# A decoder layer on one core: the output weight loads of batch 0 issued at another step, and the merge order written anew

## Chip, core and metric

One core of one Trainium2 chip. The metric is the device time of one execution in microseconds (us). Engines: PE (TensorE, matmuls), DVE (VectorE), ACT (ScalarE), POOL (GpSimd), SP (the queue that issues most DMAs).

## The reference

For 4 batches of 256 tokens by 256 channels, one decoder layer, with a layer norm behind each of its three parts:

```
x = layernorm(x + attn(x, Wqkv, Wo))        # 16 heads of 128, 2 kv heads, rotary, tanh softcap, causal
x = layernorm(x + xattn(x, ctx, mask, ...)) # 16 heads of 16, q and o projections quantised to 8 bits
x = layernorm(x + ffn(x, Wr, br, W1, W2))   # router keeps 4 of 16 blocks per token, gelu
```

## The kernel before

Each batch is cut into small operations, and they are grouped in seven streams, each in its own fixed order: `r` (rotate: split of x and weights, `rot` 0 to 8, that is k and eight pairs of q heads), `s` (scores: `near` j for each pair of heads, `far` for every two pairs), `m` (`val`, `mix` 2j and 2j + 1 for pair j, `turn` j, `proj` j, and in batch 0 `wo` n, at the end `norm1`), `c` (context, and in batch 0 `quant_w`, `turn_w` and `w1`), `x` and `y` (cross-attention of the two token tiles: `quant_x`, `turn_x`, `query`, `turn_q`, `xscore`, `turn_p`, `xmix`, `turn_o`, `quant_o`, `turn_ox`, `outproj`), `n` (`turn_z`, `route`, `turn_m`, `hidden`, `ffn`). The string `ORDER` of 531 letters merges the streams; `make_plan` takes the next operation of the stream that each letter names. Every engine, SP too, walks through the same plan and issues its own part of each operation, so the string sets the order on all of them at once. An engine waits on semaphores in that order and never passes a waiting instruction.

Work of batches overlaps: while self-attention of batch b + 1 runs, cross-attention and the network of batch b fill in.

The PE writes to 7 PSUM banks in turn (`claim`): an operation takes the bank that was used seven uses before, once that one is released by ACT or DVE. The output projection of pair j, `proj` j, adds to a bank of its own, `acc` (12 matmuls, line 585).

The output weights `Wo` come in eight parts, one for each pair. In batch 0 a part is loaded as plain f32 into one of three buffers `wo_f` (these lie in `xs`, so the profile shows the load as `xs<-in_wo`, 256 KB, line 374). At `wo` n ACT rounds it to `wo_s` (line 888), POOL takes the rest (line 1354), and SP stores both to DRAM (`wo_parts`, 512 KB, line 387), from where later batches load them. The rounding of part n (n from 3) waits for the load of part n, for the store of part n - 3 and for `proj` n - 3. The load of part n + 3 waits for the rest of part n. In the stream, `wo` 0 to 2 stand at the start and `wo` n + 3 stands right behind `proj` n.

Rotary in batch 0 is done with DVE reading across halves. From batch 1 on, DVE writes two products (lines 1046, 1047), SP swaps halves by two DMAs (line 398), and POOL adds (line 1348). POOL also does the causal masks (line 1366) and the power in each layer norm (line 1377). Line 1250 is DVE's router. Line 442 loads `W1` (1 MB).

Of the kernel before, what the change touches and what calls it, by code (L numbers as in the profile page):

```python
# [36 lines left out]
B, T, C = 4, 256, 256  # L37
# [3 lines left out]
PAIRS = NH // 2  # L41
# [15 lines left out]
WO_SLOTS, WO_FLAT = 3, 3  # L57
# [70 lines left out]
def network_ops(b):  # L128
# [16 lines left out]


ORDER = (
    "rrrrrmsmrmssrrmrrmsmmrssmsmrmmmmmmmrmssrrrmmmmmmcsssmmmmmccmmmmrrmcccccmmmcmrcmmrsrmcccssmcmmmrmmsmssrxmm"
    "rrmmmsyssmmmxmsmyxmmmmxyssmmrmmymmyyrrmymxxmmrxxxxyymmmrryxyxsxxmxyyymmyyxxxxsyyysrryxxxyymmxymxxmmsccmmx"
    "msscxyrcccxmmssrsyxmmmmmmsyxrmmmmmyyxssmmxrrxxmxmmmmmyxrynmmmrxxxyxxrxxsxyyxxmmmsyysyymmxyyyxyrynyxyysyrn"  # L150
    "xyyymmmxmxynyymcxnyxxsscnnxynccccmxmsmrxmsyxryxmxxsxxmyxsxxxxnynmxxyymxxmxyyxyyxmnxyyysyxyxmmyyyymmxyyyxs"
    "ymcymymmmmmymmymmcmmcccmmncnnnyynxxyxnyxyxnynxyxxxxxyyyyyxxxxyyyyxxxyyyxyxyyxxnyxyyxxnnnynxynxnnnnnnnnnnn"
    "nnnnnn")


# [33 lines left out]
def build_decoder(nc, x, xT, ctxT, mask, wqkv, wo, wkvT, xwq, xwo, xbias, wrT, br, w1T, w2T,  # L189
# [10 lines left out]
    with ExitStack() as ctx:  # L200
# [114 lines left out]
        def wait_for(eng, name, b, i=0, t=0):  # L315

            if b >= 0:
                eng.wait_ge(sig[name, t], count(name, b, i))
# [8 lines left out]
        def wait_filled(eng, kind, b, i=0, t=0, k=0):  # L327

            if b >= 0:
                eng.wait_ge(filled, where[kind, b, i, t, k] + 1)  # L330


        tiles = [(k, i) for k, _, i, _ in score_ops(0)]
        tile_at = {t: n for n, t in enumerate(tiles)}

# [22 lines left out]
        def _(sp):  # L358
            rows = lambda a: a.rearrange("(k p) n -> p k n", p=P)
            def load_tokens(b):  # L360
                if b == 1:
                    sp.wait_ge(quant_w, 14)
                for t in range(TT):
                    wait_for(sp, "ln2", b - 2, 1, t)
                sp.dma_start(y1[:, b % 2], rows(x[b])).then_inc(xtok_in[b % 2], 16)

            def load_wo(b, j):

                n = b * PAIRS + j
                slot = n % WO_SLOTS  # L370
                if b == 0:
                    if j >= WO_FLAT:
                        sp.wait_ge(wo_lo, j - WO_FLAT + 1)
                    sp.dma_start(wo_f[:, j % WO_FLAT], rows(wo)[:, 2 * j:2 * j + 2, :]).then_inc(wo_flat[j % WO_FLAT], 16)
                else:
                    wait_for(sp, "projected", *divmod(n - WO_SLOTS, PAIRS))
                    first = j % WO_SLOTS
                    if b == 1:
                        sp.wait_ge(wo_out[first], 16 * (j // WO_SLOTS + 1))
                        if slot != first:  # L380
                            sp.wait_ge(wo_out[slot], 16 * len(range(slot, PAIRS, WO_SLOTS)))
                    sp.dma_start(wo_s[:, slot].rearrange("p a m c -> p (a m c)").bitcast(F32), wo_parts[j]).then_inc(wo_in[slot], 16)

            def store_wo(j):

                sp.wait_ge(wo_lo, j + 1)
                sp.dma_start(wo_parts[j], wo_s[:, j % WO_SLOTS].rearrange("p a m c -> p (a m c)").bitcast(F32))\
                    .then_inc(wo_out[j % WO_SLOTS], 16)

            def swap_halves(b, i):  # L390

                n = b * (PAIRS + 1) + i
                lower, upper = slice(0, HD // 2), slice(HD // 2, HD)
                if n >= 2:
                    sp.wait_ge(sig["rotated", 0], n - 1)
                wait_for(sp, "roped", b, 3 * i)
                for dst, src in ((lower, upper), (upper, lower)):
                    sp.dma_start(rope_s[dst, n % 2], rope_t[src, n % 2]).then_inc(swapped[n % 2], 16)

            def load_context(b):  # L400
                wait_filled(sp, "ctx", b - 1, 1)
                sp.dma_start(ctx_s[:], rows(ctxT[b])).then_inc(ctx_in, 16)

            def load_mask(b):
                for t in range(TT):
                    wait_for(sp, "xmasked", b - 1, 4 * QUADS - 1, t)
                sp.dma_start(mask_s[:], rows(mask[b])).then_inc(mask_in, 16)
# [4 lines left out]
            for n in range(1, PIECES):  # L412
                sp.dma_start(raw[n], rows(wqkv[:, (n - 1) * PW:n * PW])).then_inc(piece_in[n], 16)
            sp.dma_start(ident_s[:], ident).then_inc(ident_in, 16)
            for j in range(WO_SLOTS):
                load_wo(0, j)
            load_tokens(0)
            for w, a in enumerate((xwq, xwo)):
# [9 lines left out]
            for kind, b, i, t in plan:  # L428

                done.add((kind, b, i, t))  # L430
                both = all((kind, b, i, n) in done for n in range(TT))
                if kind == "rot" and b:
                    swap_halves(b, i)
                elif kind == "rot" and i == 2 * PLAIN - 1:
                    wait_filled(sp, "rot", 0, 2 * PLAIN - 2)
                    wait_filled(sp, "val", 0)
                    wait_for(sp, "x_lo", 0)
                    sp.dma_start(xT_s[:], rows(xT[1])).then_inc(x_in, 16)
                elif kind == "rot" and i == PAIRS:
                    for n in range(PLAIN, PIECES):  # L440
                        sp.wait_ge(piece_lo[n], 2)
                    sp.dma_start(w1_f[:], rows(w1T)).then_inc(w1_in, 16)
                elif kind == "quant_w" and i == 1:
                    load_tokens(1)
                elif kind == "wo":
                    store_wo(i)
                elif kind == "proj" and b * PAIRS + i + WO_SLOTS < B * PAIRS:
                    load_wo(*divmod(b * PAIRS + i + WO_SLOTS, PAIRS))
                elif kind == "outproj" and both and b + 2 < B:
                    load_tokens(b + 2)  # L450
                elif kind == "ctx" and i == TT - 1 and b + 1 < B:
                    load_context(b + 1)
                elif kind == "xscore" and i == QUADS - 1 and both and b + 1 < B:
                    load_mask(b + 1)
                elif kind == ("last" if b == B - 1 else "ffn"):
                    wait_for(sp, "ln3", b, 4, t)
                    sp.dma_start(out[b, t * P:(t + 1) * P, :], y3[:, t, :]).then_inc(sig["stored", t], 16)
# [983 lines left out]
```

## Time and profile before

| | us |
|---|---|
| median of 3 runs | 398.35 (396.69 to 400.66) |
| profiled execution | 400.16 |
| its span, first to last instruction | 398.4 |
| PE busy | 376.6 (95%) |
| PE weight loads busy | 322.9 (81%) |
| DVE busy | 299.9 (75%) |
| ACT busy | 247.2 (62%) |
| POOL busy | 148.8 (37%) |
| mean granted TensorE clock | 0.994 of full |

The span is that of the profiled execution, and 1.8 us of its time lie outside it. Busy time of PE is modelled from its pipelined matmuls and can hide gaps shorter than one matmul.

### The profile page before, as it was taken

The page shows a single profiled execution, that of the slowest core. Times are in us where ns is not written, and L with a number is a line of the kernel's source. Part 1 is how long each engine was busy: PE and PEld are TensorE (multiplying, and loading weights), DVE is VectorE, ACT ScalarE, POOL GpSimd, SP SyncE. Part 2 cuts the span into 40 slices and gives each one's busy share as a digit, 9 for nine tenths or more (in the row PEclk, how much of TensorE's full clock was granted, in tenths as well). Part 3 has the DMA queues.
Part 4 walks back from the last instruction along what each step waited for, and adds up shares of the span by engine and source line. Part 5 has one row for each costly group of instructions (what it writes and reads, how often), then busy time and mean ns, then how long its engine had stood idle before and what let it go on. Part 6 is the DMA issues. An engine that isn't in the chain of part 4 may idle for free.

```text
span 398.4 us, 9013 instructions
## 1 busy us (share of the span) xinstructions
PE 376.6 (95%) x3038; PEld 322.9 (81%) x3038; DVE 299.9 (75%) x900; ACT 247.2 (62%) x526; POOL 148.8 (37%) x173
## 2 busy tenths in 40 slices
PE   7989998999999999998999999999999988899893
PEld 6768886878899988787998896888888877679783
DVE  2998998758778687878887888897888687777603
ACT  1666545644676984555579847598983439984230
POOL 6598545546824604245553122142113321000101
PEclk9999999999999999999999999999999999999999
DMA  7981554644335433033444110130123000000000
GB/s 266 369 294 44 171 169 149 199 150 91 119 107 134 129 112 81 26 107 128 129 143 132 30 54 28 41 105 9 62 81 100 8 2 20 8 3 2 26 2 26
DMA packets 21404, 38.42 MB, mean 96 GB/s; under 512 B 2544, under 2 KB 12144, under 8 KB 21360
## 3 DMA queue, kind: packets, MB, share of 16 engines
q1 hardware_dynamic: 20272, 36.80, 29.8%
q10 hardware_dynamic: 1088, 1.05, 0.8%
q8 instruction: 26, 0.43, 0.5%
q14 instruction: 18, 0.15, 0.1%
HBM read 25.52 MB, written 5.24 MB: 77 GB/s over the span
## 4 chain that ended last, share of the span: by engine, by line
PE 74%; DVE 7%; DMA 5%; ACT 4%; POOL 4%; issue 3%; SPq 1%; POOLq 0%; DVEq 0%; ACTq 0%
PE bank L479 10%; PE acc L585 9%; PE bank L671 7%; PE bank L552 5%; PE bank L732 5%; PE bank L529 5%; PE bank L752 5%; PE bank L683 4%; PE bank L660 4%; PE bank L611 4%; PE bank L566 3%; PE bank L555 3%; DMA rope_s<-rope_t 2%; PE bank L537 2%; DMA xs<-in_wo 2%
## 5 line engine op out<-in xcount | busy, mean ns | idle before, releaser
L914 ACT ACTIVATE xs<-xs,xneg 128x256 f32<-128x256 f32 x128 | 54.4, 500 | 9.1 <-DVE xneg L1191 8.8
L1359 POOL TENSOR_TENSOR a_lo<-a_flat,a_hi 128x512 fp32r<-128x512 f32 x32 | 41.6, 1302 | 26.7 <-ACT a_flat L829 26.7
L1377 POOL TENSOR_TENSOR small<-small,half 128x1 f32<-128x1 f32 x24 | 13.2, 550 | 101.6 <-DVE small L1077 101.6
L585 PE MATMUL acc<-wo_s,a_hi 128*128 128x256 f32 x256 | 49.8, 293 | 0.7 <-POOL a_lo L1359 0.6
L1191 DVE CUSTOM_DVE_ANT_0 xs<-bank,mask_s 128x256 f32<-128x256 f32 x128 | 46.3, 419 | 3.0 <-PE bank L660 2.7
L1348 POOL TENSOR_TENSOR q_T<-q_T,rope_s 128x512 f32<-128x512 f32 x24 | 30.8, 1285 | 45.6 <-DMA rope_s<-rope_t 45.4
L552 PE MATMUL bank<-v_s,p_near 128*128 128x129 f32 x256 | 41.7, 277 | 2.8 <-POOL p_far L1366 1.8
L585 PEld LDWEIGHTS acc<-wo_s,a_hi 128*128 128x128 f32 x256 | 39.3, 189 | 4.0 <-POOL a_lo L1359 2.8
L552 PEld LDWEIGHTS bank<-v_s,p_near 128*128 128x128 f32 x256 | 35.2, 191 | 6.7 <-issue 4.8
L479 PE MATMUL bank<-x_hi,wqkv_hi 128*128 128x256 f32 x124 | 37.6, 304 | 0.2 <-DVE q_T L1047 0.2
L585 PE MATMUL acc<-wo_s,a_lo 128*128 128x256 f32 x128 | 35.9, 281 | 0.0
L671 PE MATMUL bank<-ident_s,xs 128*128 128x128 f32 x256 | 35.2, 277 | 0.4 <-ACT xs L914 0.3
L479 PE MATMUL bank<-x_lo,wqkv_hi 128*128 128x256 f32 x124 | 34.9, 282 | 0.0
L479 PE MATMUL bank<-x_hi,wqkv_lo 128*128 128x256 f32 x124 | 34.8, 281 | 0.0
L671 PEld LDWEIGHTS bank<-ident_s,xs 128*128 128x128 f32 x256 | 28.3, 141 | 7.1 <-issue 6.2
L829 ACT CAST a_hi<-bank 128x512 fp32r<-128x512 f32 x32 | 18.8, 586 | 23.5 <-PE bank L566 23.2
L529 PE MATMUL bank<-q_T,k_T 128*128 128x512 f32 x64 | 32.8, 602 | 0.3
L870 ACT ACTIVATE p_near<-bank 128x512 f32<-128x512 f32 x32 | 19.1, 598 | 20.3 <-PE bank L529 20.0
L1200 DVE COPY xp_T<-bank 128x512 f32<-128x512 f32 x32 | 21.9, 688 | 10.2 <-PE bank L671 9.9
L829 ACT CAST qS<-bank 64x256 fp32r<-64x256 f32 x64 | 23.3, 363 | 9.4 <-PE bank L648 8.5
L1067 DVE TENSOR_TENSOR a_s<-bank,a_rec 128x256 f32<-128x256 f32 x64 | 27.2, 425 | 2.2
L660 PE MATMUL bank<-kS,qS 128*128 128x256 f32 x128 | 23.8, 309 | 2.4 <-ACT qS L829 1.5
(169 smaller groups left out, 999.0 us busy)
## 6 DMA issues: line engine op xcount, KB each, us to landing
wo_s<-wo_parts SPq DMA_DIRECT2D x24, 512.0 KB, 3.4
rope_s<-rope_t SPq DMA_DIRECT2D x54, 128.0 KB, 2.3
wo_parts<-wo_s SPq DMA_DIRECT2D x8, 512.0 KB, 3.7
xs<-in_wo SPq DMA_DIRECT2D x8, 256.0 KB, 5.7
stage<-in_wqkv SPq DMA_DIRECT2D x2, 512.0 KB, 6.3
xp_T<-in_wqkv SPq DMA_DIRECT2D x2, 512.0 KB, 8.0
y<-in_x SPq DMA_DIRECT2D x4, 256.0 KB, 3.0
ctx_s<-in_ctxT SPq DMA_DIRECT2D x4, 256.0 KB, 2.8
```

The source lines that it names most:

```text
L479: ins = mm(ps, lhs[i], rhs[j], start=(k == 0 and n == 0), stop=(last and n == 2))
L529: mm(ps[:, :], k_T[:, j // 4, 0:P], q_T[:, j % 4].rearrange("p h q -> p (h q)"), start=True, stop=True).then_inc(filled, 1)
L552: ins = mm(o, p_near[:, j % NEAR, m, t * P:(t + 1) * P], v_s[:, 0, j // 4, :], start=True, stop=(t == 0))
L585: ins = mm(acc[:, t, :], a[x], wo_s[:, slot, w, m, :], start=(j == 0 and t == 0 and m == 0 and p == 0), stop=(j == PAIRS - 1 and m == 1 an ...
L660: ins = mm(ps[m][:, m2 * T:(m2 + 1) * T], qS[:, t, m2, m, :], kS[:, g, m2, :], start=True, stop=True)
L671: ins = transpose(ps[:, m2 * T + k * P:m2 * T + (k + 1) * P], xs[:, t, m, m2, k * P:(k + 1) * P], ident_s[:])
L829: copy(dst, src).then_inc(sig[name, t], 1)
L914: activation(xs[:, t, m, m2, :], xs[:, t, m, m2, :], ACT.Exp, bias=xneg[:, t, m, m2:m2 + 1], scale=-1.0)\
L1067: v.tensor_tensor(a_s[:, j % 2, t], ps[:, :, 0:HD], rec.to_broadcast([P, 2, HD]), ALU.mult)\
L1191: do(v.tensor_tensor_reduce(out=xs[:, t, m, m2, :], in0=bank("xscore", b, g, t, m)[:, m2 * T:(m2 + 1) * T], in1=mask_s[:, t, :], scale=-1. ...
L1348: g.tensor_tensor(dst, dst, (rope_s if b else rope_t)[:, n % 2], ALU.add).then_inc(sig["rotated", 0], 1)
L1359: g.tensor_tensor(a_lo[:, j % 2], a_flat[:, j % 2], a_hi[:, j % 2].bitcast(F32), ALU.subtract)\
```

## The change

In batch 0, SP issues the load of part n + 3 in the operation `wo` n, just behind the store of part n, and no longer in the operation `proj` n. The loads of batches 1 to 3 stay at `proj`. The first three loads are issued at the start as before (`WO_FLAT` and `WO_SLOTS` are both 3). No instruction is added or removed, and no wait. `ORDER` is written anew with the same number of each letter.

```
 ORDER = (
-    "rrrrrmsmrmssrrmrrmsmmrssmsmrmmmmmmmrmssrrrmmmmmmcsssmmmmmccmmmmrrmcccccmmmcmrcmmrsrmcccssmcmmmrmmsmssrxmm"
+    "rrrrrmsmrmssrmrrsrmmmmrsssmrrmmssmmmrmmrmmsrmmmmmmmmsscmmmrrccmmmmmrmmcmcccccmmrrcssmmmsmmrrmcmmsssxmcmrr"
...
-            for j in range(WO_SLOTS):
+            for j in range(WO_FLAT):
                 load_wo(0, j)
...
                 elif kind == "wo":
                     store_wo(i)
-                elif kind == "proj" and b * PAIRS + i + WO_SLOTS < B * PAIRS:
+                    if i + WO_FLAT < PAIRS:
+                        load_wo(0, i + WO_FLAT)
+                elif kind == "proj" and PAIRS <= b * PAIRS + i + WO_SLOTS < B * PAIRS:
                     load_wo(*divmod(b * PAIRS + i + WO_SLOTS, PAIRS))
```

All five long lines of the string differ. Read through `make_plan`, the operations of batch 0 behind the first projection stand as follows (`b.i` is batch and index):

```
before: proj0.0 wo3 mix6 mix7 piece1 turn2 near5 far2 rot8 piece2 split_x1 proj1 wo4 mix8 mix9 turn3 proj2
        quant_w0 near6 near7 far3 wo5 mix10 mix11 turn4 proj3 turn_w0 quant_w1 wo6 mix12 mix13 turn5 rot1.0
        rot1.1 proj4 turn_w1 w1 x4 wo7 mix14 mix15 ctx0 turn6 rot1.2 ctx1 proj5 turn7 rot1.3 near1.0 rot1.4
        proj6 turn_k0 turn_k1 turn_k2 near1.1 far1.0 proj7 turn_k3 norm1 norm1 val1 rot1.5 ...
after:  proj0.0 wo3 rot8 mix6 mix7 piece2 turn2 proj1 near6 split_x1 wo4 mix8 mix9 turn3 proj2 wo5 mix10
        mix11 near7 far3 quant_w0 turn4 proj3 wo6 rot1.0 rot1.1 turn_w0 quant_w1 mix12 mix13 turn5 proj4 wo7
        rot1.2 mix14 mix15 turn_w1 turn6 w1 x4 ctx0 proj5 turn7 rot1.3 rot1.4 ctx1 near1.0 near1.1 proj6
        proj7 norm1 far1.0 norm1 val1 rot1.5 ...
```

In batches 1 to 3 operations move by a few places each. Near the end, `route` and `turn_m` of batch 2 move forward: before, `route` stood behind the last `turn_p` of batch 3 and `turn_m` behind both `quant_o`; after, `route` stands behind the third `xscore` of one tile of batch 3 and `turn_m` right behind the last `turn_p`. From `outproj` of batch 3 on the two orders are alike.

## Rows read from the trace of the kernel before

**Rows 1.** Busy time by stretch; columns as in the first line.
```profile
core 0: us, PE busy (x) PEld busy (x) DVE busy (x) ACT busy (x) POOL busy (x), PEclk, DMA share, GB/s
8.24:34.38 26.14, 24.88 (x135) 19.14 (x135) 23.12 (x37) 14.73 (x27) 20.09 (x18) 1.00 0.84 289
34.38:57.80 23.42, 22.73 (x167) 19.81 (x168) 21.60 (x43) 14.58 (x27) 14.92 (x14) 1.00 0.40 135
57.80:98.98 41.18, 38.94 (x260) 31.30 (x258) 30.87 (x69) 19.98 (x37) 21.61 (x23) 1.00 0.50 149
98.98:312.01 213.03, 211.82 (x1863) 184.03 (x1863) 170.61 (x557) 151.15 (x335) 78.61 (x90) 1.00 0.30 88
...
325.50:355.40 29.90, 26.02 (x248) 21.56 (x246) 22.89 (x89) 25.47 (x64) 1.10 (x2) 1.00 0.03 10
355.40:376.40 21.00, 18.92 (x160) 17.03 (x158) 14.80 (x58) 8.60 (x18) 2.19 (x4) 1.00 0.02 7
376.40:398.40 22.00, 15.51 (x90) 13.99 (x90) 4.50 (x22) 4.31 (x8) 1.09 (x2) 0.90 0.06 19
```

**Rows 2.** The chain that ended last, batch 0: start, us, what.
```profile
39.13 1.54 SPq L442
...
40.71 6.48 DMA xs<-in_wo
...
47.22 0.63 ACT wo_s L888
...
55.12 2.84 PE bank L479 x24
```

**Rows 3.** Waits, whole span: us in total, times, longest.
```profile
ACT wo_s L888 <- DMA xs<-in_wo: 14.7, 4, 5.3
```

**Rows 4.** Timeline of PE: start, us, and idle before in brackets.
```profile
50.48 0.50 PE L585 MATMUL acc<-wo_s,a_hi 128*128 128x256 f32 x2 [0.55 <-POOL a_lo L1359]
...
62.61 1.98 PE L611 MATMUL bank<-wkv_s,ctx_s 128*128 128x512 f32 x4 [1.16 <-ACT a_flat L829]
...
78.15 0.80 PE L585 MATMUL acc<-wo_s,a_hi 128*128 128x256 f32 x2
```

**Rows 5.** Timeline of SP: the DMAs as issued.
```profile
18.91 8.18 SPq L387 DMA_DIRECT2D wo_parts<-wo_s  x3
...
27.64 0.79 SPq L374 DMA_DIRECT2D xs<-in_wo  x1
```

**Rows 6.** Timeline of DVE, batch 0.
```profile
47.32 0.68 DVE L1093 TENSOR_REDUCE q_amax<-z 128x2 f32<-128x512 f32 x1
...
58.21 0.48 DVE L1117 TENSOR_SCALAR q_tmp<-ident_s,q_scale 128x128 f32<-128x128 f32 x2
...
63.59 2.92 DVE L1233 TENSOR_TENSOR w_lo<-xp_T,w_hi 128x512 fp32r<-128x512 f32 x4 [1.11 <-ACT w_hi L930]
```

**Rows 7.** The chain that ended last, start of batch 1.
```profile
74.89 0.70 DVE rope_t L1046
...
76.16 4.29 DMA rope_s<-rope_t
...
84.44 0.53 POOL small L1377
...
91.51 0.44 PE bank L566 x4
...
99.14 1.54 PE acc L585 x12
```

**Rows 8.** The chain that ended last, its end part.
```profile
355.41 0.81 PE bank L710 x8
356.25 0.17 DVE prob L1250
...
358.36 0.19 DVE keep L1266
...
376.39 4.59 PE bank L732 x24
```

More of the change, by code:

```diff
@@ L147 @@
 ORDER = (
-    "rrrrrmsmrmssrrmrrmsmmrssmsmrmmmmmmmrmssrrrmmmmmmcsssmmmmmccmmmmrrmcccccmmmcmrcmmrsrmcccssmcmmmrmmsmssrxmm"
[L149 to L152, printed above, removed]
+    "rrrrrmsmrmssrmrrsrmmmmrsssmrrmmssmmmrmmrmmsrmmmmmmmmsscmmmrrccmmmmmrmmcmcccccmmrrcssmmmsmmrrmcmmsssxmcmrr"
+    "rcmmmscssmxymmmmmyxmmsysmxsyxmmmmrrmxmmyyxxryyyxxmmmmmymyxxxyyyyxxxymmmmxmysxxssryyrryxxxsymymxycrsxxmmsm"
+    "rcxmmxxmmsccccssyrrymmxmmmsmyxsmymsmmymxmmmrmyxrmxmxxxmyxxmmmrynmyyrxxysxyxyymmxyxxmmsysyyxyxyrrmmxxyyyrn"
+    "xyysymmxysxyyccxnmnnyxncynsxmnxcccxsymmsxsmxmxmxmxyxxrxyxxxnxyxnsyyxxmxmmyyyryxyyxxyyynxyymmyyxmxssmmmmxy"
+    "yyxmymmymymmcymmycmmmmnccyccnnnyxnyxxnxyxynynyxxyyyxxyyyynxxxxyyyxxxyyyxxxyyxxxnyxyynxnynxxynxnnnnnnnnnnn"
     "nnnnnn")
```

## The prediction

> **What bounds the kernel now.** I read the busy time of each engine by stretch first, then the chain that ended last, then the waits of ACT and PE in batch 0, then SP's issues. The stretches [rows 1] show PE idle for 1.2 of 213.0 us between the first projection of batch 1 (98.98) and the last two of batch 3 (312.01). Idle time elsewhere is 1.3 us up to 34.38, 0.7 up to 57.80, 2.2 up to 98.98, and 3.9, 2.1 and 6.5 in the last three stretches. So the time is PE's work, plus what PE loses in batch 0, plus what it loses behind the last projection.
>
> Busy time can hide short gaps, so I also added up PE's work along the plan, at the duration that an undisturbed group of each kind has in the chain: 0.12 us for a matmul of a rotation or a projection (24 in 2.84 [rows 2]), and likewise for the others. PE's first real matmul starts at 8.24. Against this sum PE is 0.6 us late at projection 0 of batch 0 (34.38 [rows 1]), 1.4 at projection 3 (50.48 [rows 4]), 3.8 at projection 7 (78.15 [rows 4]), 5.6 at projection 0 of batch 1 (99 [rows 7]), and 4.7 at the last projection of batch 3 (the difference of 0.9 is the error of the sum). So some 5.0 us are lost between 34 and 99, nothing that I can see from 99 to 312, and the rest behind it.
>
> The Trainium skill (Perfetto Trace Analysis, Identifying the Most-Contended Engine) says that matmul busy time is a bad measure of how full TensorE is, and that weight load busy time should be taken. By that, the middle has 29 us of room (184.0 of 213.0), and a better order could win some of it there. The sum of the plan's work speaks against it here, and only a small chance below rests on it.
>
> **The loads.** ACT waits four times for a part of the output weights, 14.7 us in all [rows 3]. The worst case is in the chain [rows 2]: behind the store of part 3 the load of W1 holds SP for 1.54 us from 39.13, the load of part 4 lands 6.48 us after 40.71, ACT rounds at 47.22, and projection 3, whose input was queued on ACT behind that rounding, starts at 50.48 [rows 4]. After the change, loads 3, 4 and 5 go out behind stores 0, 1 and 2, that is between 19 and 27; before, load 3 went at 27.64 [rows 5], load 4 at 40.7 and load 5 after it. Load 6 goes out behind store 3 (about 39) and ahead of W1, load 7 behind store 4 (about 45). Roundings 4 to 7 are due at about 43, 46, 51 and 58, right behind projections 1 to 4. Each load then has 6 us or more, so this wait goes, all 14.7 us of it.
>
> What the loads collide with: the DMA engines are 84% busy up to 34 [rows 1], so the three early loads land later than one alone would, and delay the x of batch 1, which no engine reads before 40. The price is between 0 and 2 us of a transfer with over 10 us to spare; I take 0. SP's queue gets no new wait: the load needs the same rest of part n that the store just before it waited for.
>
> **What PE gets of it.** ACT is not the bound. PE itself idled only 0.55 us ahead of projection 3 and 1.16 us ahead of the first context product, whose bank was held by ACT's late copy [rows 4]. DVE idled 1.11 us for ACT's late rounding of W1 [rows 6]. The direct gain is 0.55 + 1.16 = 1.7 us.
>
> What is late next is DVE. Up to 57.80 it is busy 21.6 of 23.4 us [rows 1]. The two quantisations of weights, some 5 us each, lie between 47.32 and 58.7 [rows 6], and everything on DVE behind them waits. In the new order two rotations of batch 1 (1.2 us each) come ahead of the second one, and mix 12 and 13 follow it. Counted on from the measured end of mix 9, DVE ends quantisation 1 at about 61.0 and mix 13 at 62.1, while PE asks for them at 60.4 and 61.0. PE waits some 1.1 us there, with 0 and 2.5 us as bounds: 2.5 if both added rotations (2.4 us) come on top. Before, that place cost nothing.
>
> Then the start of batch 1. Before, rotation 3 runs on DVE at 74.89, its swap lands 4.29 us after the issue at 76.16, POOL adds, masks, and only then does the first power of layer norm 1 at 84.44 [rows 7]; the norm holds DVE, rotation 5 follows, and its bank holds PE, which comes to turn 0 of batch 1 at 91.51 [rows 7]. This is where PE goes from 3.8 to 5.6 us late. In the new order rotation 2 stands 6.9 us of DVE work earlier, ahead of the W1 rest and the context, projections 6 and 7 come together (at about 74 to 75.5 in place of 78.2), and fewer operations lie between projection 7 and the norm. Counting the same steps: rotation 4 on DVE ends at 73 to 75, its swap and POOL's addition at 79 to 81.3, the power at 80.2 to 82.5 in place of 84.44, and PE reaches turn 0 of batch 1 at 88 to 90, where it was at 91.51 with 0.9 us more work behind it. That is 0.6 to 2.6 us less lost. I take the middle, **1.6 us**, for the whole of batch 0; the bounds with full success or none are 5.0 and 0.
>
> **The first 34 us.** The new order moves near 2 ahead of rotation 6 and a weight split ahead of mix 4. DVE is busy 23.1 of 26.1 us there [rows 1], and its work up to projection 0 is 2.0 us more, PE's is 1.7 us more. I take 0, bounds 1 us either way.
>
> **The middle, 99 to 312.** The same work, and PE has nothing to win. It can lose: the shortest distance between a rotation and its first score, in PE work, was 6.8 us from batch 1 on, and is now 5.8 and 5.9 us in batch 2, while the chain of rotation, swap, addition takes 6 to 8 us by [rows 7]. Bounds 0 and 1.9, I take 0.3, since in the trace the waits of this kind leave PE idle for only 1.2 us in all of this stretch.
>
> **The end.** From 325.5 to 355.4 ACT is busy 25.5 of 29.9 us, the fullest engine but PE, and PE idles 3.9 us [rows 1]. The route of batch 2 now comes into this stretch. Its PE part (0.81 us [rows 8]) fits into PE's idle time, and what PE lost to the router by the sum of its work, 0.76 us, is gone from 358: 1.6 us, less 0.5 us since the last mix now follows its copy more closely, gives 1.1. In return the router's DVE steps, 356.25 to 358.55 [rows 8], and ACT's two small exponentials (between DVE's steps, some 0.5 us) come into the busy stretch: between 0.5 us (only ACT's part) and 4.0 us (2.3 us of DVE, and 1.7 us in which DVE waits for four exponentials ahead of the router's on ACT). I take 1.1, so 0 in sum, with bounds -0.6 and +2.9. The clock is another term: 24 matmuls of batch 3's network took 4.59 us at 376.39 against 2.84 for as many at full clock, and the granted clock is 0.90 in this stretch against 1.00 before [rows 1, 2, 8]. PE had idled 2.1 of the 21.0 us ahead of it. The end of the order is unchanged, so I take it as it is, 1.75 us either way.
>
> **The sum.** -1.6 + 0.3 = -1.3 us against the profiled execution of 400.16 (its span of 398.4 and 1.8 around it), which makes 398.9; that execution is 1.8 above the median, so against the median of 398.35 it makes **397.0 us**.
>
> **Rivals.**
> - The wait moves to DVE. The loads are early, but the quantisations and the two rotations ahead of mix 12 cost what the loads gave (the 2.5 bound), and the norm is reached no sooner. For it: DVE's 21.6 of 23.4 us. Against it: rotations 2 to 4 do come earlier. It gives 398.35. To it belongs the case that the change doesn't do what it says (a load still last at a rounding), which gives the same time.
> - All of batch 0's loss goes. -5.0, and -1.1 at the end if the route is hidden: 392.3. For it: every chain through ACT is shorter by 4 to 5 us, and the rotations of batch 1 by more. Against it: DVE's load. The skill's rule of room in the middle is part of this case.
> - Slower: the router of batch 2 on DVE, ahead of the scores of batch 3. Its price is up to +2.9 us net, and it decides from the point where the early gain is below it. With the gain at its least, 0, and 1 us in the first stretch or the middle, this makes 398.35 + 3.9 = 402.2; with the forecast gain, 399.9.
>
> **How the numbers follow.** Forecast 0.46 (own range 395.5 to 398.0), wait moved to DVE 0.20, all gone 0.20, slower 0.14. The range leaves out 2 in 10: from 392.3 with half of the second rival at its end to 401.2, between the two times of the third: 392.5 to 401.2. A measurement here tells some 1% from no change (4 us; three runs spread over 4.0). Faster by over 1%, below 394.4, is nearly all of the second rival and a tail of the forecast: 0.22. Slower by over 1%, above 402.3, needs the third at its full price: 0.08. Within 1%: 0.70.
>
> **What would show it.** Loads of parts 3 to 5 on SP before 28; ACT's wait for them gone; projection 3 starting at about 49.7; no idle time ahead of the first context product, but some 1 us at turn 6 or turn_w 1, released by DVE; the first power of norm 1 near 81; projection 0 of batch 1 at about 97.4; the middle as long as before; ACT's stretch ahead of 355 longer and the router's wait at 358 gone. I am wrong if PE's idle time in batch 0 doesn't shrink, if the middle has waits of several us, or if the end grows by more than 2 us.

## The result and the profile after

The changed kernel takes 393.85 us (median of 6 runs, 392.26 to 395.3), the kernel before on the same chip 397.88 (6 runs, 396.57 to 400.66). The ratio is 0.9896, 95% interval 0.9866 to 0.9927: 4.0 us faster. The forecast was 397.0, in a range of 392.5 to 401.2 that holds the result. The sign was right; the gain was forecast at 1.3 us, a third of what came. The result lies below the forecast's own range (395.5 to 398.0) and in that of the second rival, all of batch 0's loss gone, which had a chance of 0.20.

The profiled execution of the changed kernel took 395.3 us, its span is 393.6. Busy time by stretch answers to [rows 1]. The first two stretches are cut at the times of [rows 1], not at events (in this execution PE starts at 9.22 and projection 0 of batch 0 at 37.71); 96.66 is projection 0 of batch 1, 308.03 the last two projections of batch 3, and the last line is the end part. In the kernel before, the last two projections start at 311.45, so the fourth line of [rows 1] is 0.56 us longer than this one's counterpart:

```profile
8.24:34.38 26.14, 24.82 (x119) 18.66 (x120) 21.73 (x35) 14.24 (x26) 17.84 (x17) 0.93 0.91 309
34.38:57.80 23.42, 23.42 (x180) 20.89 (x179) 21.03 (x44) 15.57 (x29) 18.23 (x16) 1.00 0.41 147
57.80:96.66 38.86, 38.35 (x263) 31.37 (x262) 33.13 (x78) 19.61 (x36) 21.84 (x23) 1.00 0.50 144
96.66:308.03 211.37, 211.14 (x1862) 183.81 (x1861) 165.93 (x548) 149.34 (x333) 77.49 (x88) 1.00 0.30 87
...
372.00:393.60 21.60, 14.20 (x92) 12.59 (x92) 5.58 (x26) 5.16 (x9) 1.09 (x2) 0.96 0.06 19
```

PE has no idle time at all between 34.38 and 57.80, where it had 0.7 us, and 0.5 us from there to batch 1, where it had 2.2. ACT works 15.6 us in that stretch where it worked 14.6, and POOL 18.2 where it worked 14.9: both have done more by 57.80 (ACT 29.8 against 29.3 us, POOL 36.1 against 35.0). The view of waits has no line in which ACT's rounding waits for a load [rows 3]. SP's timeline shows why, and answers to [rows 5]:

```profile
21.43 0.34 SPq L387 DMA_DIRECT2D wo_parts<-wo_s  x1
21.81 0.43 SPq L374 DMA_DIRECT2D xs<-in_wo  x1
...
25.32 0.44 SPq L374 DMA_DIRECT2D xs<-in_wo  x1
...
29.62 1.06 SPq L374 DMA_DIRECT2D xs<-in_wo  x1
...
43.14 0.43 SPq L374 DMA_DIRECT2D xs<-in_wo  x1
43.67 0.78 SPq L442 DMA_DIRECT2D xp_T<-in_w1T  x1
```

Loads 3, 4 and 5 go out at 21.8, 25.3 and 29.6, each behind a store, and load 6 goes ahead of W1. PE's timeline has one wait between 34 and 97, and none at turn_w 1. The kernel before has four: 0.55 and 1.16 us [rows 4], and two at the start of batch 1, 0.74 at 84.58 (for POOL's mask of `far`) and 0.20 at 88.93:

```profile
65.80 0.50 PE L587 MATMUL acc<-wo_s,a_hi 128*128 128x256 f32 x2 [0.44 <-POOL a_lo L1361]
```

In the chain of work that ended last, the first power of norm 1, the last piece ahead of projection 0 of batch 1, and the 24 matmuls of batch 3's network answer to [rows 7] and [rows 8]:

```profile
80.26 0.53 POOL small L1379
...
96.37 0.86 PE bank L539 x2
...
373.08 3.04 PE bank L734 x24
```

Against the same sum of PE's work as in the prediction, PE is now 2.3 us late at projection 0 (37.71), 2.3 at projection 3 (51.29), 3.2 at projection 5 (65.80), 3.3 at projection 0 of batch 1 (96.66). So 1.0 us is lost between these two ends, where the kernel before lost 5.0.

The changed execution began badly: its first weights let PE start at 9.22, not 8.24, and the granted clock is 0.93 up to 34 (1.00 before). In two other runs that share its first operations (e3, e11 below) PE starts at 8.13 and 8.34, and projection 0 stands at 35.07 and 35.28. The span before was 398.4, so the 4.8 us between the spans are +1.7 (start), -4.0 (34 to batch 1), -1.1 (middle, 211.4 against 212.5), -1.4 (end, where the 24 matmuls above are 1.55 us shorter than 4.59 [rows 8]).

The profiled execution of the kernel before is 2.3 us above its median, that of the changed kernel 1.5 above its own. So e1 below, which has the time and the order of the kernel before, is the fairer trace to compare with.

### The profile page after: what moved, and what is told of

It reads as the page before. It is cut to its first block, busy times and chain, and to the rows that moved or that the text cites. A ratio compares the mean times of both kernels' runs of the same rounds, so it can differ in the third digit from the quotient of the medians.

```text
span 393.6 us, 9011 instructions
## 1 busy us (share of the span) xinstructions
PE 376.1 (96%) x3038; PEld 322.4 (82%) x3038; DVE 295.4 (75%) x900; ACT 245.4 (62%) x524; POOL 149.8 (38%) x173
## 4 chain that ended last, share of the span: by engine, by line
PE 75%; DVE 9%; DMA 5%; issue 3%; POOL 3%; ACT 3%; SPq 1%; POOLq 0%; DVEq 0%; ACTq 0%
PE acc L587 9%; PE bank L481 8%; PE bank L673 6%; PE bank L554 6%; PE bank L734 6%; PE bank L531 6%; PE bank L754 5%; PE bank L685 4%; PE bank L662 3%; PE bank L568 3%; PE bank L557 3%; DMA rope_s<-rope_t 3%; PE bank L539 3%; PE bank L613 2%; PE bank L500 2%
## 5 line engine op out<-in xcount | busy, mean ns | idle before, releaser
L1048 DVE TENSOR_TENSOR rope_t<-bank,sin_s 128x512 f32<-128x512 f32 x27 | 18.6, 688 | 10.9 <-PE bank L481 6.3
```

## The experiments

All are whole kernels timed in five rounds, with ratios to the kernel before. `ORDER` is shown as operations. Lines of kernels with the early loads stand two below those of before.

**e1: the loads alone.** The order of before, the loads of the changed kernel.

```
 ORDER = (the string before)
+                    if i + WO_FLAT < PAIRS:
+                        load_wo(0, i + WO_FLAT)
```

> The merge order of before, with the loads of parts 3 to 5 issued behind the first stores. Theory A (the gain of 4 us needs both parts: PE loses some 4 us less between 34 and 99, of which only the waits for ACT belong to the loads): 1.7 us faster than before, ratio 0.996, within 0.993 to 0.999; ACT no longer waits for a load, the idle 0.55 and 1.16 us of PE are gone, DVE's quantisations still hold mix 10 and 11. Rival B (the loads alone do it): ratio 0.990. Rival C (the order alone does it): ratio 1.000.

Measured 398.05 us, ratio 1.0008 (0.9979 to 1.0037). Nothing is gained: the time that rival C named, and below what the loads should have given by theory A. ACT waits for no load any more, and the idle times ahead of projection 3 and of the first context product are gone. In their place stand two that the kernel before did not have, at turn_w 0:

```profile
52.68 0.38 PE L599 MATMUL bank<-identb_s,q_int 128*128 128x128 bf16 x4 [1.31 <-DVE q_int L1106]
54.09 0.68 PE L605 MATMUL bank<-q_tmp,ones 128*128 128x128 f32 x4 [1.02 <-DVE q_tmp L1119]
```

PE is stopped by quantisation 0 on DVE: it got 1.71 us and paid 2.33. DVE and POOL side by side, same execution:

```profile
49.12 0.37 DVE L1097 TENSOR_SCALAR q_scale<-q_amax 128x2 f32<-128x2 f32 x1
...
51.16 1.37 DVE L1106 TENSOR_SCALAR q_int<-q_tmp 128x512 bf16<-128x512 f32 x1
52.57 1.37 DVE L1119 TENSOR_SCALAR q_tmp<-ident_s,q_scale 128x128 f32<-128x128 f32 x2
...
57.39 0.43 DVE L1104 TENSOR_SCALAR q_tmp<-q_tmp 128x512 f32<-128x512 f32 x1
```

```profile
50.82 1.44 POOL L1356 TENSOR_TENSOR wo_s<-xs,wo_s 128x512 fp32r<-128x512 f32 x1
52.22 1.44 POOL L1361 TENSOR_TENSOR a_lo<-a_flat,a_hi 128x512 fp32r<-128x512 f32 x1
```

The two DVE instructions that lie beside POOL's take 1.37 us each; where POOL is idle the first kind takes 0.43 and the second 0.48 for both (changed kernel, 59.90 and 60.36). In the kernel before, too, a pair of POOL's rests (weights, then attention) lies on quantisation 0, at 47.91 and 49.14. With the loads early that pair comes sooner and stretches the DVE instruction ahead of the quantisation instead, so that it starts 1.1 us later (48.41 against 47.32 [rows 6]), and the next pair, shown above, falls on its end:

```profile
45.67 1.75 DVE L1026 TENSOR_TENSOR x_lo<-xT_s,x_hi 128x512 fp32r<-128x512 f32 x1
```

```profile
45.16 1.71 POOL L1356 TENSOR_TENSOR wo_s<-xs,wo_s 128x512 fp32r<-128x512 f32 x1
46.83 1.72 POOL L1361 TENSOR_TENSOR a_lo<-a_flat,a_hi 128x512 fp32r<-128x512 f32 x1
```

In the kernel before, the same x_lo takes 0.68 us at 45.65, with POOL idle. Projections 3, 5 and 7 stand at 49.70, 67.61 and 78.17 here and at 50.48, 67.60 and 78.15 before: what is won ahead of projection 3 is lost at turn_w 0.

**e2: the order alone.** The order of the changed kernel, loads at the projection.

```
 ORDER = (the string after)
-                    if i + WO_FLAT < PAIRS:
-                        load_wo(0, i + WO_FLAT)
```

> The merge order of after, with the loads of batch 0 at the projections as before. Theory A: the roundings of parts 4 to 7 wait for loads again, and in this order projections 1 and 2 leave less time; most of the gain is gone, ratio 0.996 to 1.003. Rival B: 1.000. Rival C: 0.990, since the rotations and projections of the start of batch 1 still come earlier.

Measured 400.71 us, ratio 1.008 (1.0052 to 1.0108), slower. ACT waits 15.9 us for loads, and PE idles 1.67 us at 50.47 and 3.19 us at 68.83:

```profile
68.83 0.79 PE L585 MATMUL acc<-wo_s,a_hi 128*128 128x256 f32 x2 [3.19 <-POOL a_lo L1359]
```

So neither part gains alone, and together they gain 1.04%: the two need each other. Rival B falls with e1 and rival C with e2; theory A, that both parts are needed, stands, but not its figures, since by them the loads alone would have given 1.7 us.

**e3 and e4: where in the order.** e3 has the early loads, the first 158 operations of the new order and the rest of the old one; e4 is the changed kernel with its last 67 operations in the old order.

```
e3: ORDER = after[:158] + before[158:]
e4: ORDER = after[:464] + before[464:]
```

> Loads early, the order of after for the first 158 operations (up to projection 4 of batch 1), that of before from there on. Theory A: batch 0 holds nearly all of the gain, ratio 0.990 to 0.993. Rival D (the middle, where PE's idle time fell from 1.2 to 0.2 us, or the end gave part of it): ratio 0.994 or more, and less than after by over 1 us.

> The kernel of after, with only the last 67 operations (from turn_z of batch 2 on) in the order of before, so that the route of batch 2 stands behind the last turn_p again. Theory A (the moved route costs as much as it gives): same as after, ratio 0.990 with 0.5 us to either side. Rival D: the moved route helps, ratio 0.994; or it costs, as the slower rival of the prediction had it, ratio 0.985.

Measured 394.33 us, 0.9925 (0.9899 to 0.9952), and 394.27 us, 0.9918 (0.9892 to 0.9945). The start carries some three quarters of the gain. What is left, 0.3% to the middle and the end together (e3) and 0.2% to the end alone (e4), lies within the intervals.

**e5 and e6: finer.** Early loads with the first 57 operations (to projection 3) or 83 operations (to near 0 of batch 1) of the new order.

```
e5: ORDER = after[:57] + before[57:]
e6: ORDER = after[:83] + before[83:]
```

> Loads early, the order of after for the first 57 operations (up to projection 3 of batch 0; the first quantisation stands behind mix 11 in it), that of before from there on. Theory A2 (with early loads PE is held by DVE's first quantisation, between mix 9 and mix 10, and its turn_w; the gain is in the place of that and of the rotations, in batch 0): PE no longer idles 2.3 us at turn_w 0; ratio 0.996. Theory D2 (the start of batch 1 or later gives it all): 1.000, as with the loads alone.

> Loads early, the order of after for the first 83 operations (up to near 0 of batch 1, rotations 0 to 4 of batch 1 at their new places), that of before from there on. Theory A2: all of the gain but what the norm's new place gives: ratio 0.991 to 0.994. Theory D2: 0.998 or more.

Measured 396.44 us, 0.9945 (0.9917 to 0.9974), and 396.29 us, 0.9959 (0.9933 to 0.9984). Up to projection 3 the new order turns e1's nothing into half of the gain: quantisation 0 starts at 47.67 there instead of 48.41 and the two instructions that took 1.37 us each take 0.43 and 0.73, so PE idles 0.56 us at turn_w 0 in place of 2.33. e6 missed what was expected of it (0.991 to 0.994): the operations 58 to 83, with the rotations of batch 1 at their new places, give nothing more, and PE idles 0.49, 0.57 and 1.62 us there (63.31, 71.40, 74.70), the longest for DVE's `parts` (line 1151). The other 0.3% comes in the step from 83 to 158 operations (projections 6 and 7, the norm and the start of batch 1); the intervals of e6 and e3 overlap, and no run divides this step further.

**e7 and e8: only rotations moved.** On the early loads and the old order, e7 puts rotations 0 and 1 of batch 1 right behind projection 3, e8 puts rotation 2 right behind projection 4.

```
-proj3 turn_w0 quant_w1 wo6 mix12 mix13 turn5 rot1.0 rot1.1 proj4 turn_w1 ...
+proj3 rot1.0 rot1.1 turn_w0 quant_w1 wo6 mix12 mix13 turn5 proj4 turn_w1 ...       (e7)
-proj4 turn_w1 w1 x4 wo7 mix14 mix15 ctx0 turn6 rot1.2 ctx1 ...
+proj4 rot1.2 turn_w1 w1 x4 wo7 mix14 mix15 ctx0 turn6 ctx1 ...                     (e8)
```

> Loads early, the order of before, with only rotations 0 and 1 of batch 1 moved ahead of turn_w 0 and quantisation 1, so that PE has 2.8 us of other work while DVE quantises. Theory A2: the 1.3 and 1.0 us that PE idles at turn_w 0 with the loads alone go, some 1 us may come back where mix 12 and 13 now stand behind them on DVE: ratio 0.994 to 0.998. Theory D2: 1.000.

> Loads early, the order of before, with only rotation 2 of batch 1 moved ahead of turn_w 1, the rest of W1 and the context. If the late rotations (swap, POOL's addition, masks, the norm's power behind them) are what costs PE 1.8 us at the start of batch 1: ratio 0.996. If not, 1.000.

Both expectations failed: 402.63 us, 1.0099 (1.0061 to 1.0137), and 399.57 us, 1.0044 (1.0015 to 1.0073). In e7 the waits at turn_w 0 are gone as expected, but PE idles 5.56 and 0.81 us at turn_w 1, where only some 1 us was expected to come back. The DVE timeline of e7 over quantisation 1, and POOL's:

```profile
59.18 1.69 DVE L1102 TENSOR_SCALAR q_tmp<-y,q_rs 128x256 f32<-128x256 f32 x2
60.90 1.40 DVE L1104 TENSOR_SCALAR q_tmp<-q_tmp 128x512 f32<-128x512 f32 x1
62.33 1.37 DVE L1106 TENSOR_SCALAR q_int<-q_tmp 128x512 bf16<-128x512 f32 x1
63.74 1.36 DVE L1119 TENSOR_SCALAR q_tmp<-ident_s,q_scale 128x128 f32<-128x128 f32 x2
```

```profile
59.46 1.26 POOL L1350 TENSOR_TENSOR k_T<-k_T,rope_s 128x512 f32<-128x512 f32 x1 [5.59 <-DMA rope_s<-rope_t]
60.76 1.26 POOL L1350 TENSOR_TENSOR q_T<-q_T,rope_s 128x512 f32<-128x512 f32 x1
61.98 1.44 POOL L1356 TENSOR_TENSOR wo_s<-xs,wo_s 128x512 fp32r<-128x512 f32 x1
63.38 1.44 POOL L1361 TENSOR_TENSOR a_lo<-a_flat,a_hi 128x512 fp32r<-128x512 f32 x1
```

Four DVE instructions in a row take 1.4 to 1.7 us, each beside one of POOL's. The rotations sent their swaps off early, and POOL's additions came back 4.3 us later (from the first product on DVE at 55.14) on top of quantisation 1, which took 7.0 us (58.06 to 65.1) where the changed kernel takes 3.2 (57.66 to 60.84). My theory that the place of the rotations alone is the gain falls. e8 keeps e1's waits of 1.31 and 1.02 us at turn_w 0, and its clock is lower (0.94 from 34 to 58).

**e9: the suspected cost taken away.** e1, with POOL's instructions beside the quantisations made short: they compute 8 columns of each half of 256, and the kernel leaves out the rest, so its output is not the layer's.

```
+                n = 8 if j in (4, 5, 6) else C
+                g.tensor_tensor(s[:, 1, :, 0:n], wo_f[:, j % WO_FLAT, :, 0:n], s[:, 0, :, 0:n].bitcast(F32), ...
...
+                n = 8 if b == 0 and j in (3, 4, 5) else T
+                g.tensor_tensor(a_lo[:, j % 2, :, 0:n], a_flat[:, j % 2, :, 0:n], a_hi[:, j % 2, :, 0:n]...
```

> e1_loads_only with one thing left out: in batch 0 POOL's rests of output weight parts 4 to 6 and of attention pairs 3 to 5 are computed for 8 columns of each half in place of 256 (the other columns keep what stood in the buffer), so POOL's instructions of 1.27 to 1.72 us beside the two quantisations of weights shrink. No other engine has an instruction more or less, and the order is that of before. Theory (POOL's tensor-tensor work beside DVE stretches the quantisation, and PE waits for it at turn_w 0): the two DVE instructions that took 1.37 us each beside POOL's (quotient to integers, diagonal of scales) fall to about 0.5, quantisation 0 ends near 52 in place of 53.8, PE's 1.31 + 1.02 us ahead of turn_w 0 are gone, ratio to before 0.992 to 0.996. Rival (the quantisation is late by its place in the order, behind the split and the context of pair 3, and POOL is a bystander): its instructions keep their length, PE's wait stays near 2.3 us, ratio 0.999 to 1.002.

Measured 394.15 us, ratio 0.9914 (0.988 to 0.9948). The order is that of before to the letter, and 0.9% appears. PE has 0.1 us of idle time from 34 to 80, and 0.46 us from there to 98. The same DVE instructions and POOL's:

```profile
50.08 0.43 DVE L1106 TENSOR_SCALAR q_int<-q_tmp 128x512 bf16<-128x512 f32 x1
50.54 0.88 DVE L1119 TENSOR_SCALAR q_tmp<-ident_s,q_scale 128x128 f32<-128x128 f32 x2
```

```profile
51.11 0.22 POOL L1357 TENSOR_TENSOR wo_s<-xs,wo_s 128x16 fp32r<-128x16 f32 x1
```

Quantisation 0 ends at 51.4 in place of 53.9, quantisation 1 takes 3.2 us in place of 4.3. The trace accounts for some half of the gain: from projection 0 of batch 0 to that of batch 1 it takes 60.9 us against 62.9 in e1. The medians are 3.9 us apart, but this profiled execution, at 396.15, is the longest of its nine.

**e10: more cover for quantisation 1.** e7, with turn_w 1 and the W1 rest moved behind mix 15.

```
-turn5 proj4 turn_w1 w1 x4 wo7 mix14 mix15 ctx0 ...
+turn5 proj4 wo7 mix14 mix15 turn_w1 w1 x4 ctx0 ...
```

> e7_rot01_ahead with turn_w 1 and the split of W1 moved behind mix 15, as in the changed kernel, so that quantisation 1, which took 7 us there beside POOL's work, is not asked for by PE until some 5 us of PE work later. Theory (rotations 0 and 1 ahead of turn_w 0 pay once both quantisations have PE work to cover them): PE's idle of 5.56 + 0.81 us at turn_w 1 is gone or below 1 us, quantisation 0 is covered too, ratio 0.992 to 0.997. Rival (the rotations themselves, or POOL's additions of them, are what delays; cover only moves the wait to mix 12 to 15): PE idles several us at turn 6 or at a projection, ratio 1.002 to 1.010.

Measured 401.78 us, ratio 1.0109 (1.0055 to 1.0163). Missed. PE's wait at turn_w 1 is halved, not gone, and the time stays where the rival put it (1.002 to 1.010) or just above:

```profile
61.50 0.38 PE L599 MATMUL bank<-identb_s,q_int 128*128 128x128 bf16 x4 [1.22 <-DVE q_int L1106]
63.93 1.19 PE L605 MATMUL bank<-q_tmp,ones 128*128 128x128 f32 x4 [2.04 <-DVE q_tmp L1119]
```

Its last quantisation step takes 2.39 us at 61.39, beside POOL's additions at 61.19 and 62.44, and the granted clock is 0.92 from 57.8 to 80. Rotation 2 (24 matmuls, 2.84 us [rows 2]) stands ahead of turn_w 1 in the new order and not in e10; that it is the missing cover I argue from its length, no run shows it.

**e11: quantisation 0 put back.** The changed kernel, quant_w 0 ahead of wo 5 as before.

```
-proj2 wo5 mix10 mix11 near7 far3 quant_w0 turn4 proj3 ...
+proj2 quant_w0 wo5 mix10 mix11 near7 far3 turn4 proj3 ...
```

> The changed kernel with one operation moved back: quant_w 0 stands right behind projection 2, ahead of wo 5 and mix 10, as in the kernel before, in place of behind far 3. All of the rest is the changed kernel. Theory (what the new order gained in batch 0 hangs on where the quantisations fall beside POOL's rests): quantisation 0 grows from 3.9 towards 5 us, the mixes 10 and 11 and turn 4 come behind it, PE idles 1 to 2 us there, ratio to before 0.992 to 0.997, so 0.3 to 0.6% behind the changed kernel. Rival (the gain lies in the rotations and the start of batch 1): ratio 0.988 to 0.991, as the changed kernel.

Measured 394.5 us, ratio 0.9916 (0.9889 to 0.9944). Quantisation 0 grows to 4.6 us (46.08 to 50.64), but PE waits for it nowhere: the two rotations ahead of turn_w 0 cover it. Between the two theories' figures, and within the interval of the changed kernel: the place of this one operation is not the gain; by the two ratios 0.2% would hang on it, which the intervals do not show.

**e12: the same cost taken away from the changed kernel.** The edit of e9 on the new order.

```
 ORDER = (the string after)
+                n = 8 if j in (4, 5, 6) else C
+                n = 8 if b == 0 and j in (3, 4, 5) else T
```

> The changed kernel with the same thing left out as in e9_small_rests: POOL's rests of output weight parts 4 to 6 and attention pairs 3 to 5 of batch 0 computed for 8 columns of each half in place of 256. There, on the order of before, it took the ratio from 1.0008 to 0.9914. Theory (the new order has already moved the two quotations of time away: in it POOL's rests stand beside other DVE work, and PE waits for no quantisation): there is almost nothing left for it to win, ratio to before 0.986 to 0.990, at most 0.3% ahead of the changed kernel. Rival (smaller rests help by their own length, since a projection comes sooner after its rest, whatever the order): it wins here what it won there, ratio 0.979 to 0.983.

Measured 394.83 us, ratio 0.9928 (0.9901 to 0.9955), above the 0.986 to 0.990 of the theory and far from the rival. What was worth 0.9% on the old order is worth nothing on the new one (0.3% behind the changed kernel; the intervals overlap). That speaks against the reading that e9 gained because a projection comes sooner after a shorter rest. The traces give a reason why it may even cost a little: the store of part 6 no longer holds the swaps on SP, they go out at 52.70 instead of 56.81, and POOL's additions come back at 55.95 and 58.39, inside quantisation 1 (4.9 us, 55.08 to 59.98), and PE idles 0.46 us at turn_w 1 (60.58):

```profile
55.95 1.29 POOL L1350 TENSOR_TENSOR k_T<-k_T,rope_s 128x512 f32<-128x512 f32 x1 [3.99 <-DMA rope_s<-rope_t]
58.39 1.31 POOL L1350 TENSOR_TENSOR q_T<-q_T,rope_s 128x512 f32<-128x512 f32 x1 [1.15 <-DMA rope_s<-rope_t]
```

In the changed kernel they come at 62.01, just behind its end, because the store of part 6 holds SP until 56.7 (5.56 us for two stores from 51.15). The prediction did not count on that, so a part of the short quantisation 1 is luck:

```profile
62.01 1.27 POOL L1350 TENSOR_TENSOR k_T<-k_T,rope_s 128x512 f32<-128x512 f32 x1 [5.66 <-DMA rope_s<-rope_t]
```

```profile
60.36 0.48 DVE L1119 TENSOR_SCALAR q_tmp<-ident_s,q_scale 128x128 f32<-128x128 f32 x2
...
63.31 0.69 DVE L1048 TENSOR_TENSOR rope_t<-bank,sin_s 128x512 f32<-128x512 f32 x1 [1.39 <-POOL k_T L1350]
```

## Why the prediction was right in sign and short in size

**The loads.** Right as a mechanism: ACT's 14.7 us of waits are gone, none of the four is left. Load 5 went out at 29.6, where all three were to go before 28; with the start in time (e3) it went at 27.0.

**What PE gets of it (1.7 us).** This step was wrong as a gain of its own: it took PE's idle time as time won, and did not count what PE would meet next. e1 has exactly that part, both idle times go, and the time stays. The first rival, that the wait moves to DVE, is what the loads alone do; it moves to turn_w 0, which the old order asks for too soon.

**DVE late next (+1.1 us at turn 6 or turn_w 1).** It did not come. I had DVE end quantisation 1 at 61.0 and mix 13 at 62.1, and it ended them at 60.8 and 61.9. But the changed execution started late, so that PE did not ask for turn_w 1 before 62.32. In e3, which has the same order there and no late start, quantisation 1 ends at 58.2 and PE asks at 59.67, also without a wait. The reason is the length of the quantisations, which I took from the trace of before (some 5 us each) as fixed. They are not: 5.1 and 4.7 us there, 3.9 and 3.2 in the changed kernel. In the trace of before the surplus could be read, with POOL's timeline beside DVE's:

```profile
48.03 1.19 DVE L1095 TENSOR_SCALAR q_scale<-q_amax 128x2 f32<-128x2 f32 x1
...
49.46 1.53 DVE L1100 TENSOR_SCALAR q_tmp<-z,q_rs 128x256 f32<-128x256 f32 x2
```

```profile
47.91 1.28 POOL L1354 TENSOR_TENSOR wo_s<-xs,wo_s 128x512 fp32r<-128x512 f32 x1 [2.74 <-ACT wo_s L888]
49.14 1.29 POOL L1359 TENSOR_TENSOR a_lo<-a_flat,a_hi 128x512 fp32r<-128x512 f32 x1
```

A scale of two numbers for each partition takes 1.19 us because it ends when POOL's instruction does (49.2); alone it takes 0.17. The Trainium skill (SBUF — State Buffer, Who interferes with whom) says that a VectorE instruction of certain kinds and a GpSimd instruction take a shared pair of ports as a lock, so the second one stands until the first has ended. The traces agree: DVE's instructions take 1.19 us (before), 1.37 (e1), and 1.40 and 1.37 (e7), beside POOL's of 1.28, 1.44, 1.26 and 1.44; in e9, where POOL's are short, the one that took 1.37 takes 0.43. The prediction didn't weigh this rule, and should have.

**Start of batch 1.** Right, and near its better end: the power of norm 1 at 80.26 (80.2 to 82.5 forecast, 84.44 before) and projection 0 at 96.66 (97.4 forecast), though the execution started 1.7 us late. Against PE's work, the whole of batch 0 behind projection 0 gave 4.0 us, where I took 1.6, the middle of 0.6 to 2.6, with outer bounds of 0 and 5.0. This is the mis-sized term. Two things are in it. First, 1.7 of the 5.0 us that I counted as lost were this one execution: e1, with the same order, has projection 7 at the same time (78.17 against 78.15), but projection 0 of batch 1 at 97.30 in place of 98.98. The swap of rotation 3, issued in both at 75.7, came back sooner there, and POOL's addition with it, in e1 and before:

```profile
79.05 1.29 POOL L1350 TENSOR_TENSOR q_T<-q_T,rope_s 128x512 f32<-128x512 f32 x1 [1.19 <-DMA rope_s<-rope_t]
```

```profile
80.58 1.29 POOL L1348 TENSOR_TENSOR q_T<-q_T,rope_s 128x512 f32<-128x512 f32 x1 [2.75 <-DMA rope_s<-rope_t]
```

So the loss of 1.8 us at the start of batch 1, from 3.8 to 5.6, on which the prediction built its gain, was almost all scatter: from projection 7 to projection 0 of batch 1 the kernel before takes 20.8 us, and e1, e7, e9 and e10, with the same operations there, take 19.1 to 20.3. Second, measured from e1, the stretch from projection 0 to projection 0 gave 2.3 us in the changed kernel and 2.7 in e3 (62.9 us against 58.95 and 58.5, with 1.7 us of PE's work moved ahead of it), at the better end of 0.6 to 2.6. I had set it in the middle because DVE's load stood against more, and that load was in part waiting for POOL.

**The first 34 us.** Taken as 0 within 1 us. The changed execution was 1.7 us worse, by its start and clock, so the bounds missed; e3, with the same operations and no late start, comes to projection 0 at 35.07, 0.7 us later than before with 1.7 us more of PE's work done. So the order gained some 1.0 us there, at the bound, and the bad start hid it. With the 2.7 us of the paragraph above that makes the 3.7 us by which the medians of e1 and e3 differ: e3's whole gain is made ahead of projection 0 of batch 1, and the sum had 1.6 for it.

**The middle.** Forecast +0.3, and the trace has -1.1: PE's idle time fell from 1.2 to 0.2 us. That is no gain of the order. e1, with the order of before, takes 211.3 us for the same stretch, and e3, with the order of before from projection 4 of batch 1 on, takes 212.7, so one order spreads over more than this difference. The closer scores of batch 2 cost nothing that shows. The changed order also has two of ACT's table loads (ACT_TABLE_LOAD, 1.28 us each) fewer, 8 against 10 (two between 238 and 260, where the kernel before has four); PE waits for none of them there. The 29 us of room that weight load busy time promised there stay unfound: weight loads are busy 183.8 of 211.4 us, and PE idles 0.2.

**The end.** Taken as 0, and it is: from the last two projections 85.6 us against 86.95, and the clock's 1.55 is all of that. The router's move showed no price (e4 against the changed kernel: 0.2%, within the intervals), so nothing here speaks for the slower rival. Of the two signs named, PE's wait for the router (0.30 us at 358.68) is gone, but ACT's busy stretch did not grow: 25.1 of 29.9 us (322.2 to 352.1) against 25.5. The clock of the profiled executions went by chance: the 24 matmuls took 3.04 to 3.07 us in three of the fourteen kernels of this case (changed, e3, e6) and 4.4 to 4.6 in the others, over both ends of the order. The six runs of the changed kernel alone have mean granted clocks of 0.993 to 0.999.

What stays open: which operation between 83 and 158 gives the other part of the gain, whether the 0.3% between e3 and the changed kernel is there at all, and whether e10 is any better than e7 (its span is 2.4 us shorter, 399.5 against 401.9, the medians 401.78 and 402.63, the intervals overlap).

## What to carry to other kernels

A wait that is removed is worth what the next engine lets through. Here it was nothing until the work behind it was laid out anew, and the new layout alone made the kernel slower. Two edits that lose or gain nothing one by one can gain together. Before taking the duration of a DVE instruction as fixed, look whether it has the same duration everywhere; where it has not, lay POOL's timeline beside it, since moving either engine changes both. And a step forward of a rotation also moves what comes back from it, in e7 POOL's additions 4.3 us later. Before building a forecast on a loss read from one trace, look whether another execution of the same order shows it; here 1.7 of 5.0 us did not come again.

## What the runs showed of the hardware

- A DVE instruction of TENSOR_SCALAR, from SBUF to SBUF, that starts while POOL runs a TENSOR_TENSOR ends with it or some 0.3 us behind it: 0.17 us becomes 1.19, 0.43 becomes 1.37 to 1.51 (1.51 in e1 at 57.85), the pair of 0.48 becomes 1.36 to 1.39, and 2.39 in e10, where POOL runs two in a row beside it. DVE's difference of two tiles in SBUF (x_lo) takes 1.75 us beside POOL in e1 and 0.68 with POOL idle (before). DVE's products with one input in PSUM kept their 0.42 us beside POOL (e1, 48.07, where POOL is busy until 48.55).
- The DMAs that swap the halves (128 KB each) land 2.2 us after their issue at the least and 2.3 in the median of 54; the longest took 4.4 us in the kernel before and 3.1 in e1, which has the same order.
- Long idle times of PE were followed by a lower clock in the same stretch: 0.85 from 57.8 to 80 in e2 (3.19 us of idle) and in e7 (5.56 and 0.81), 0.92 in e10 (1.22 and 2.04), 1.00 in the kernel before (1.16). It is no sure sign: e1 and e8 have the same idle times at turn_w 0 (1.31 and 1.02) and clocks of 1.00 and 0.94 from 34 to 58. e7 reaches projection 0 of batch 1 5.7 us later than e1, with 4.0 us more of idle time at turn_w 0 and 1, so its loss is more than its wait.
